# A deformable convolution with one signal for each corner of an item instead of one for each instruction

## The chip, the core and the metric

The kernel runs on one core of one Trainium2 chip. Its time is the device time of one execution in microseconds; 1330.88 us is the median of the three runs of the kernel before. The core has five engines that run their own instruction streams and tell each other of finished work by counters (semaphores): TensorE (PE, its weight loads PEld), VectorE (DVE), ScalarE (ACT), GpSimd (POOL) and SyncE (SP). An instruction can add one to a counter when it ends (here called a signal), and can wait until a counter has reached a value.

## The reference: what is computed

The input x is 4 images of 128 channels, 48 by 48, in float32. Layer 0 is a deformable 3x3 convolution behind a group normalisation, with a batch normalisation, a ReLU and a residual addition; layer 1 is a plain 3x3 convolution behind a second group normalisation, with a residual addition.

```python
x = x + _L0_conv_ref(_gn(x), ...)      # deformable convolution
x = x + _L1_conv_ref(_gn(x), ...)      # plain 3x3 convolution

# inside _L0_conv_ref, for 9 taps k and every output position
om = conv3x3(x, w_offset) + b_offset   # 27 channels: 9 dy, 9 dx, 9 masks
mask = sigmoid(om[:, 18:])
py = dy + (row + ky - 1);  px = dx + (column + kx - 1)
y0, x0 = floor(py), floor(px);  ly, lx = py - y0, px - x0
cols = corner(y0, x0, (1-ly)*(1-lx)) + corner(y0, x0+1, (1-ly)*lx) \
     + corner(y0+1, x0, ly*(1-lx))   + corner(y0+1, x0+1, ly*lx)
cols = cols * mask
out = einsum('bckhw,ock->bohw', cols, wk) + b_conv
y = relu(gamma * (out - mean) / sqrt(var + eps) + beta)   # mean, var over images and positions
```

## The kernel before, in words

The 4 x 2304 positions of layer 0 are cut into 24 **chunks** of 384 positions, each of three tiles of 128 positions (a tile's positions lie on the 128 partitions). The work of a chunk is cut into 9 **items**. In chunks 1 to 22 an item is one tap with its three tiles; in the first and the last chunk it is one tile with three taps (the last has ten). A pair of tap and tile is a **unit**, so an item has three units.

One unit passes through these steps:

- POOL gathers, by an indirect DMA (line 299), 128 rows of 4 x 128 floats from a table in DRAM: the four corners of every position, 256 KB. The row numbers come from `idx`.
- ACT multiplies the first corner by its weight into the PSUM buffer `PA` (`scale_item`, line 557, signal `scaled`).
- DVE adds the other three corners with their weights (`lerp_item`, line 770, signal `lerped`): corners 1 and 2 back into `PA`, corner 3 into `acc` in SBUF. It goes corner by corner and, in each, unit by unit, so that an item is nine instructions; each of the last six waits for the signal of the same unit's corner before.
- PE turns the 128x128 result round (`turn_item`, line 403, signal `turned`) into the PSUM buffer `TP`.
- ACT copies the three turned tiles to `cols` (`copy_cols`, line 538, signal `copied`).
- PE multiplies them with the weights of the tap into `CO` (`conv_item`, line 392, signal `conved` once an item).

The buffers `PA`, `TP` and `cols` are double, `acc` is triple. The order on each engine is fixed by the loops. ACT runs, for item k, `scale_item(k)` and then `copy_cols(k-1)`. DVE runs `lerp_item(k)`. PE runs `turn_item(k)` and then `conv_item(k-1)`. In the first three items of a chunk PE also computes, ahead of the turn, three taps of the next chunk's offset convolution (line 352, 27 channels into `OMT`).

The next chunk's row numbers come out of the present chunk's middle: after item 3 PE turns the offsets (line 361), and after `lerp_item(4)` DVE runs `indices` (lines 708 to 744), 18 small instructions that give `idx` (line 717), the corner weights `wt` and the sums `vsum`. POOL waits for `idx` before it gathers the next chunk's 27 units; each of its gathers also waits until the same place of `g` has been used (`lerped`). After item 1 ACT copies the previous chunk's output (`copy_out`, line 548), which waits for `conved`. `copy_cols` waits for `turned` of its item and for `conved` of the item two before (line 537), since it overwrites that item's half of `cols`. `copy_v` (line 530) copies a small transposed tile to `vt` after item 6 and also waits for `conved`.

After the last chunk come the batch statistics, the ReLU, the second normalisation and layer 1 (lines 477 and 860 to 871).

## Time and profile before

| what | value |
|---|---|
| median of 3 runs (lowest, highest) | 1330.88 us (1327.02, 1339.39) |
| the profiled execution's own time | 1331.31 us |
| its span | 1329.6 us |
| PE busy | 783.9 us (59%) |
| DVE busy | 687.7 us (52%) |
| POOL busy | 669.0 us (50%) |
| ACT busy | 369.8 us (28%) |
| mean granted TensorE clock | 0.721 of full speed |

No engine is busy for more than 59% of the span. Such a kernel is bound by the chain of who waits for whom, and not by the work of one engine, so the views that matter are those of the waits and of the order in time.

### The profile page before, as it was taken

Reading aid. Unit: us, or ns where it says so; the run is one execution under the profiler, and the core shown is the slowest. Engines: PE = TensorE matmul, PEld = TensorE weight load, DVE = VectorE, ACT = ScalarE, POOL = GpSimd, SP = SyncE. Lnnn points to the kernel's source line nnn. Section 1 sums busy time; section 2 is a strip of 40 time slices with the busy share of each in tenths; the row PEclk is TensorE's granted clock in tenths of the full one; section 3 lists DMA queues with packets and bytes.
Section 4 is the critical chain, followed back from the end, with each engine's and each line's share of the span. In section 5 each row is a group of like instructions: output and inputs, shape, how many; then the busy total and the mean of one; then the engine's idle time right before and its main releaser. Section 6 shows DMA issues by size and latency. Waiting matters only on the chain.

```text
span 1329.6 us, 10583 instructions
## 1 busy us (share of the span) xinstructions
PE 783.9 (59%) x2380; PEld 376.8 (28%) x2380; DVE 687.7 (52%) x2662; ACT 369.8 (28%) x1026; POOL 669.0 (50%) x731
## 2 busy tenths in 40 slices
PE   7463646655555544656555544656555556555999
PEld 4232222222122222222122122222122122135777
DVE  4337446446447446446437536536436436465664
ACT  3213224223213214313213214313213213234320
POOL 4374374373473474374464465364364364361743
PEclk8665766767766767767776767767777677666999
DMA  7364464363473374373474364374364364360011
GB/s 282 118 183 126 118 199 117 111 201 108 119 206 108 116 209 117 104 208 108 116 204 114 117 197 129 99 199 120 104 203 123 107 198 127 104 176 22 37 53 54
DMA packets 55971, 181.50 MB, mean 137 GB/s; under 512 B 10980, under 2 KB 11492, under 8 KB 55524
## 3 DMA queue, kind: packets, MB, share of 16 engines
q0 software_dynamic: 51840, 169.91, 44.4%
q1 hardware_dynamic: 3780, 10.32, 2.1%
q10 hardware_dynamic: 288, 0.59, 0.1%
q14 instruction: 43, 0.35, 0.1%
q8 instruction: 20, 0.33, 0.1%
HBM read 176.06 MB, written 4.72 MB: 136 GB/s over the span
## 4 chain that ended last, share of the span: by engine, by line
another core or an unknown queue 27%; PE 22%; issue 21%; DVE 19%; ACT 10%; DMA 1%; POOL 1%; ACTq 0%; DVEq 0%; SPq 0%
DVE PA L770 10%; ACT PA L557 8%; PE OMT L352 5%; PE CO L392 5%; DVE acc L770 5%; PE TP L403 4%; PE TP L477 2%; PE PA L477 2%; PE CO L477 2%; ACT cols L538 1%; PE OMT L477 1%; PE VU L477 1%; DMA g<-corner_table,idx 1%; DVE bst L688 1%
## 5 line engine op out<-in xcount | busy, mean ns | idle before, releaser
L299 POOL DMA_INDIRECT g<-corner_table,idx x648 | 612.7, 946 | 581.4 <-DVE idx L717 366.2
L770 DVE SCALAR_TENSOR_TENSOR PA<-g,wt,PA 128x128 f32<-128x128 f32 x1296 | 358.0, 349 | 496.4 <-ACT PA L557 300.0
L403 PE MATMUL TP<-ident,acc 128*128 128x128 f32 x648 | 157.4, 367 | 398.4 <-DVE acc L770 216.8
L392 PE MATMUL CO<-cols,wcs 128*128 128x384 f32 (+1 forms) x504 | 266.1, 637 | 130.0 <-issue 100.1
L538 ACT ACTIVATE cols<-TP 128x384 f32<-128x384 f32 (+1 forms) x217 | 104.9, 484 | 736.8 <-remote 364.3
L403 PEld LDWEIGHTS TP<-ident,acc 128*128 128x128 f32 x648 | 90.2, 178 | 533.7 <-DVE acc L770 280.7
L352 PE MATMUL OMT<-xn,woff 128*27 128x384 f32 (+2 forms) x450 | 231.0, 671 | 1.2 <-ACT mask L519 0.7
L770 DVE SCALAR_TENSOR_TENSOR acc<-g,wt,PA 128x128 f32<-128x128 f32 x648 | 191.5, 342 | 63.5 <-DVE acc L770 36.5
L557 ACT ACTIVATE PA<-g,wt 128x128 f32<-128x128 f32 x648 | 203.3, 358 | 9.8 <-DMA g<-corner_table,idx 8.9
L392 PEld LDWEIGHTS CO<-cols,wcs 128*128 128x128 f32 x504 | 109.8, 279 | 160.1 <-issue 113.6
L352 PEld LDWEIGHTS OMT<-xn,woff 128*27 128x27 f32 x450 | 55.7, 138 | 177.7 <-issue 174.9
L245 POOL TENSOR_TENSOR g<-xn 128x288 f32<-128x288 f32 (+1 forms) x60 | 41.9, 731 | 34.3 <-ACT xn L623 33.2
L378 PE MATMUL CO<-vt,ut 9*128 9x384 f32 (+1 forms) x56 | 32.2, 666 | 0.0
L237 POOL TENSOR_TENSOR x<-x,o 128x576 f32<-128x576 f32 x8 | 11.5, 1454 | 23.1 <-ACT o L617 23.0
L530 ACT ACTIVATE vt<-VU 9x384 f32<-9x384 f32 x24 | 11.5, 478 | 32.4 <-issue 15.1
L367 PE MATMUL VU<-ident,vsum 128*9 128x128 f32 x72 | 17.7, 374 | 2.6 <-issue 2.6
L523 ACT ACTIVATE std<-OMT,eps 128x1 f32<-128x1 f32 x5 | 1.3, 261 | 59.4 <-PE OMT L335 59.4
L519 ACT ACTIVATE mask<-OMT 128x27 f32<-128x27 f32 (+2 forms) x25 | 4.8, 192 | 46.0 <-DVE pos L709 43.2
L548 ACT ACTIVATE o<-CO,params 128x384 f32<-128x384 f32 x23 | 13.2, 575 | 13.2 <-remote 12.8
L477 PE MATMUL OMT<-g,w 128*128 128x288 f32 x48 | 14.6, 444 | 2.2 <-DVE g L245 2.2
L496 ACT ACTIVATE xn<-x,gshift,gscale 128x1872 f32<-128x1872 f32 (+3 forms) x9 | 10.8, 1236 | 17.8 <-DVE gshift L682 11.1
L367 PEld LDWEIGHTS VU<-ident,vsum 128*9 128x9 f32 x72 | 9.1, 128 | 20.1 <-issue 18.6
(119 smaller groups left out, 495.7 us busy)
## 6 DMA issues: line engine op xcount, KB each, us to landing
g<-corner_table,idx POOLq DMA_INDIRECT x648
out_dram<-x SPq DMA_DIRECT2D x16, 288.0 KB, 2.1
x<-x_dram SPq DMA_DIRECT2D x3, 1152.0 KB, 8.1
wconv<-wconv_dram SPq DMA_DIRECT2D x1, 576.0 KB, 5.2
w<-w_dram SPq DMA_DIRECT2D x1, 576.0 KB
x<-x_dram ACTq DMA_DIRECT2D x1, 384.0 KB, 5.0
x<-x_dram SPq DMA_DIRECT2D x1, 384.0 KB, 4.7
x<-x_dram ACTq DMA_DIRECT2D x1, 192.0 KB, 3.5
```

Of the source, the lines that this page charges most:

```text
L245: return eng.tensor_tensor(mixed[:, m, first:first + rows, :], p, q, op)
L299: pl.indirect_dma_start(out=g[:, k, t].rearrange("p q c -> p (q c)"), out_offset=None, in_=tab_d, in_offset=bass.IndirectOffsetOnAxis(ap=i ...
L352: last = nc.tensor.matmul(OM[:, first * W:(first + rows) * W], woff[:, k, :], xn[:, row + k // 3:row + k // 3 + rows, k % 3:k % 3 + W], st ...
L367: last = nc.tensor.transpose(VT[:, t * P:(t + 1) * P], vsum[:, t, :], ident[:])
L378: nc.tensor.matmul(co_bank(c, t)[:, lo:hi], ut[:, c // CHUNKS % 2, :], vt[:, lo:hi], start=True, stop=False)
L392: last = nc.tensor.matmul(co_bank(c, t)[:, t * P:t * P + size], wcs[:, c // CHUNKS % 2, k, :], cols[:, s % 2, n * P:n * P + size], start=F ...
L403: last = nc.tensor.transpose(TP[s % 2][:, n * P:(n + 1) * P], acc[:, s % 3, n, :], ident[:])
L477: last = nc.tensor.matmul(MX[h % 2][m][:, 0:HB], w, mixed[:, m, r:r + BR, :], start=(ky == 0), stop=(ky == 2))
L538: nc.scalar.activation(cols[:, s % 2, 0:size], TP[s % 2][:, 0:size], ACT.Copy).then_inc(copied, 1)
L557: nc.scalar.activation(PA[s % 2][:, n * P:(n + 1) * P], g[:, k, t, 0, :], ACT.Copy, scale=wt[:, c % 2, 0, t, k:k + 1]).then_inc(scaled, 1)
L688: nc.vector.bn_stats(bst[:, j, :], x[:, b * HW + j * CP:b * HW + (j + 1) * CP]).then_inc(stats_in, 1)
L770: nc.vector.scalar_tensor_tensor(acc[:, s % 3, n, :] if q == 3 else a, g[:, k, t, q, :], wt[:, c % 2, q, t, k:k + 1], a, ALU.mult, ALU.add ...
```

## The change

The change cuts the number of signals and of the waits that go with them. No arithmetic instruction is added or dropped.

- `lerp_item` signals once for each corner of an item (3 signals) and no longer once for each instruction (9). A corner's first instruction waits for the last instruction of the corner before. Over the kernel the `lerped` signals go from 1944 to 651.
- `scale_item` signals once an item (`scaled`, from 648 to 217).
- `conv_item` signals once a chunk, with the last tap, and once a tile in the last chunk (`conved`, from 217 to 26). `copy_cols` and `copy_v` no longer wait for `conved`: PE works in order, so the turn for which they wait implies the multiplication before it.
- `indices` signals in 6 steps where it had 15 (12 for the first part); `edge`, `inside` and `vm` are computed ahead of the weights `wt`.
- `copy_v(1)` moves from chunk 0's item 7 to chunk 1's item 0.

```diff
             def conv_item(c, i):
...
-                last.then_inc(conved, 1)
+
+                if k == TAPS - 1 and (c == ALL - 1 or t == TILES - 1 or len(runs) == 1):
+                    last.then_inc(conved, 1)
 
             def turn_item(c, i):
...
-                pe.wait_ge(lerped, units_before(c, i + 1) * LERP)
+                pe.wait_ge(lerped, (s + 1) * LERP)
...
             def copy_v(c):
                 act.wait_ge(v_turned, c + 1)
-                if c:
-
-                    act.wait_ge(conved, first_item(c - 1) + (1 if c - 1 not in BY_TILE else (TILES - 1) * len(TAP_SETS) + 1))
...
             def copy_cols(c, i):
...
+
                 act.wait_ge(turned, s + 1)
-                if s > 1:
-                    act.wait_ge(conved, s - 1)
...
             def copy_out(c):
-                act.wait_ge(conved, first_item(c + 1))
+                act.wait_ge(conved, c + 1)
...
             def scale_item(c, i):
...
-                    act.wait_ge(lerped, (units_before(c, i - 1) if i else units_before(c - 1, len(items(c - 1)) - 1)) * LERP)
+                    act.wait_ge(lerped, (s - 1) * LERP)
                 for n, (k, t) in enumerate(items(c)[i]):
-                    nc.scalar.activation(PA[s % 2][:, n * P:(n + 1) * P], g[:, k, t, 0, :], ACT.Copy,
-                                         scale=wt[:, c % 2, 0, t, k:k + 1]).then_inc(scaled, 1)
+                    last = nc.scalar.activation(PA[s % 2][:, n * P:(n + 1) * P], g[:, k, t, 0, :], ACT.Copy, scale=wt[:, c % 2, 0, t, k:k + 1])
+                last.then_inc(scaled, 1)
...
-                    if ahead and k == 7:
+                    if ahead and k == 7 and c:
                         copy_v(c + 1)
+                    if c == 1 and k == 0:
+
+                        copy_v(1)
...
             def lerp_item(c, i):
...
-                dve.wait_ge(scaled, done + len(units))
+                dve.wait_ge(scaled, s + 1)
                 for q in range(1, 4):
+                    if q > 1:
+                        dve.wait_ge(lerped, s * LERP + q - 1)
+                    if q == 3 and s > 2:
+                        dve.wait_ge(turned, s - 2)
                     for n, (k, t) in enumerate(units):
-                        if q > 1:
-                            dve.wait_ge(lerped, done * LERP + (q - 2) * len(units) + n + 1)
-                        if q == 3 and n == 0 and s > 2:
-                            dve.wait_ge(turned, s - 2)
                         a = PA[s % 2][:, n * P:(n + 1) * P]
-                        nc.vector.scalar_tensor_tensor(acc[:, s % 3, n, :] if q == 3 else a, g[:, k, t, q, :],
-                                                       wt[:, c % 2, q, t, k:k + 1], a, ALU.mult, ALU.add).then_inc(lerped, 1)
+                        last = nc.vector.scalar_tensor_tensor(acc[:, s % 3, n, :] if q == 3 else a, g[:, k, t, q, :],
+                                                              wt[:, c % 2, q, t, k:k + 1], a, ALU.mult, ALU.add)
+                    last.then_inc(lerped, 1)
```

In `indices` the instructions stay the same 18; the order on DVE in chunk 1 is shown from `rest` on, with the first rows of the item behind it. Before:

```order
L721 TENSOR_SCALAR rest<-less_frac 128x54 [waits index_step]
L723 TENSOR_TENSOR my<-mask,rest 128x27 [waits mask_ready,index_step]
L725 SCALAR_TENSOR_TENSOR my<-mask,less_frac 128x27
L730 TENSOR_TENSOR wt<-my,rest 128x27 [waits index_step]
L728 SCALAR_TENSOR_TENSOR wt<-my,less_frac 128x27
L730 TENSOR_TENSOR wt<-my,rest 128x27
L728 SCALAR_TENSOR_TENSOR wt<-my,less_frac 128x27
L739 TENSOR_SCALAR edge<-pos 128x54
L740 SCALAR_TENSOR_TENSOR inside<-pos,edge 128x54 [waits index_step]
L741 SCALAR_TENSOR_TENSOR vm<-inside,mask 128x27 [waits index_step]
L744 SCALAR_TENSOR_TENSOR vsum<-inside,vm 128x27 [waits v_turned,index_step]
L770 SCALAR_TENSOR_TENSOR PA<-g,wt,PA 128x128 [waits scaled,gathered5]
```

The same place of DVE in the changed kernel, as far as the end of the item behind the indices:

```order
L710 TENSOR_SCALAR rest<-less_frac 128x54 [waits index_step]
L713 SCALAR_TENSOR_TENSOR inside<-pos,edge 128x54
L717 TENSOR_TENSOR my<-mask,rest 128x27 [waits index_step,mask_ready]
L718 SCALAR_TENSOR_TENSOR my<-mask,less_frac 128x27
L720 SCALAR_TENSOR_TENSOR vm<-inside,mask 128x27
L727 TENSOR_TENSOR wt<-my,rest 128x27 [waits index_step]
L725 SCALAR_TENSOR_TENSOR wt<-my,less_frac 128x27
L732 SCALAR_TENSOR_TENSOR vsum<-inside,vm 128x27 [waits v_turned]
L757 SCALAR_TENSOR_TENSOR PA<-g,wt,PA 128x128 [waits scaled,gathered5]
L757 SCALAR_TENSOR_TENSOR PA<-g,wt,PA 128x128 [waits lerped]
L757 SCALAR_TENSOR_TENSOR acc<-g,wt,PA 128x128 [waits turned,lerped]
```

`inside` and `vm` have moved ahead of the weights (the second pair of `wt` rows, which repeats the first, is not shown), four waits are left in these rows where there were six, and each corner of the item has one wait.

On ACT, at the border of chunks 0 and 1 (item 7 of chunk 0 to item 1 of chunk 1), the copy of `vt` moves. Before:

```order
L538 ACTIVATE cols<-TP 128x384 [waits conved,turned]
L530 ACTIVATE vt<-VU 9x384 [waits conved,v_turned]
L557 ACTIVATE PA<-g,wt 128x128 [waits lerped,gathered8]
L557 ACTIVATE PA<-g,wt 128x128 [waits lerped,gathered0,wt_ready]
L557 ACTIVATE PA<-g,wt 128x128 [waits lerped,gathered1]
L548 ACTIVATE o<-CO,params 128x384 [waits conved]
```

The changed kernel, the same stretch of ACT:

```order
L550 ACTIVATE PA<-g,wt 128x128 [waits lerped,gathered8]
L531 ACTIVATE cols<-TP 128x384 [waits turned]
L550 ACTIVATE PA<-g,wt 128x128 [waits lerped,gathered0,wt_ready]
L524 ACTIVATE vt<-VU 9x384 [waits v_turned]
L550 ACTIVATE PA<-g,wt 128x128 [waits lerped,gathered1]
L541 ACTIVATE o<-CO,params 128x384 [waits conved]
```

The copy of `vt` now stands after chunk 1's first products, and of ACT's waits for `conved` only the one of `copy_out` is left.

## Rows read from the trace of the kernel before

**Rows 1.** The page: busy, 40 slices of POOL, and lines (count | busy us, mean ns)

```profile
PE 783.9 (59%) x2380; PEld 376.8 (28%) x2380; DVE 687.7 (52%) x2662; ACT 369.8 (28%) x1026; POOL 669.0 (50%) x731
...
POOL 4374374373473474374464465364364364361743
...
L299 POOL DMA_INDIRECT g<-corner_table,idx x648 | 612.7, 946 | 581.4 <-DVE idx L717 366.2
```

**Rows 2.** Waits of the whole span: engine, line <- releaser: total us, times, longest

```profile
POOL g L299 <- DVE idx L717: 366.2, 23, 18.1
ACT cols L538 <- remote: 364.3, 38, 17.6
```

**Rows 3.** Timeline, POOL: start, us, instruction, count, idle before

```profile
364.53 0.94 POOL L299 DMA_INDIRECT g<-corner_table,idx  x1 [15.49 <-DVE idx L717]
...
397.01 0.95 POOL L299 DMA_INDIRECT g<-corner_table,idx  x1 [0.30 <-issue]
414.60 0.94 POOL L299 DMA_INDIRECT g<-corner_table,idx  x1 [16.65 <-DVE idx L717]
```

**Rows 4.** That chunk in stretches: PE, PEld, DVE, ACT, POOL, clock, DMA share

```profile
366.00:374.00 8.00, 5.24 (x16) 3.04 (x17) 7.27 (x29) 2.11 (x7) 6.17 (x7) 0.60 0.67 200
374.00:400.00 26.00, 12.81 (x28) 4.05 (x28) 7.60 (x27) 3.78 (x12) 18.17 (x20) 0.70 0.74 211
400.00:414.00 14.00, 10.70 (x30) 3.89 (x30) 8.07 (x33) 5.36 (x17) 0.00 (x0) 0.69 0.00 1
```

**Rows 5.** Timeline, PE and ACT, early in that burst of gathers

```profile
368.62 0.90 PE L403 MATMUL TP<-ident,acc 128*128 128x128 f32 x3 [3.90 <-DVE acc L770]
...
369.56 0.49 ACT L538 ACTIVATE cols<-TP 128x384 f32<-128x384 f32 x1 [3.46 <-issue]
```

**Rows 6.** Timeline, PE, ACT and DVE, late in that burst

```profile
377.69 0.79 PE L403 MATMUL TP<-ident,acc 128*128 128x128 f32 x3 [2.56 <-DVE acc L770]
378.66 0.49 ACT L538 ACTIVATE cols<-TP 128x384 f32<-128x384 f32 x1 [3.54 <-PE TP L403]
383.58 0.35 DVE L770 SCALAR_TENSOR_TENSOR acc<-g,wt,PA 128x128 f32<-128x128 f32 x1 [1.03 <-DVE acc L770]
387.10 0.55 PE L403 MATMUL TP<-ident,acc 128*128 128x128 f32 x3 [2.28 <-remote]
391.28 0.49 ACT L538 ACTIVATE cols<-TP 128x384 f32<-128x384 f32 x1 [11.29 <-remote]
391.67 0.94 ACT L557 ACTIVATE PA<-g,wt 128x128 f32<-128x128 f32 x3
402.59 0.49 ACT L538 ACTIVATE cols<-TP 128x384 f32<-128x384 f32 x1 [9.98 <-remote]
```

**Rows 7.** The chain of waits there: start, us, what (L537 waits for conved)

```profile
382.89 0.02 ACTq L537
...
396.89 0.02 ACTq L537
```

**Rows 8.** Timeline, DVE and ACT, late in the next burst

```profile
435.06 0.35 DVE L770 SCALAR_TENSOR_TENSOR PA<-g,wt,PA 128x128 f32<-128x128 f32 x1 [3.52 <-remote]
436.46 0.35 DVE L770 SCALAR_TENSOR_TENSOR PA<-g,wt,PA 128x128 f32<-128x128 f32 x1 [1.04 <-issue]
...
446.26 0.49 ACT L538 ACTIVATE cols<-TP 128x384 f32<-128x384 f32 x1 [16.77 <-remote]
```

**Rows 9.** Timeline, DVE, after the burst of rows 3

```profile
411.13 1.65 DVE L770 SCALAR_TENSOR_TENSOR PA<-g,wt,PA 128x128 f32<-128x128 f32 x6 [1.44 <-ACT PA L557]
412.69 0.86 DVE L770 SCALAR_TENSOR_TENSOR acc<-g,wt,PA 128x128 f32<-128x128 f32 x3
...
414.15 0.19 DVE L717 SCALAR_TENSOR_TENSOR idx<-low,row 128x27 int32<-128x27 f32 x1
```

**Rows 10.** Timeline, the first burst: PE and ACT

```profile
29.87 0.90 PE L403 MATMUL TP<-ident,acc 128*128 128x128 f32 x3 [1.25 <-DVE acc L770]
...
45.74 0.49 ACT L538 ACTIVATE cols<-TP 128x384 f32<-128x384 f32 x1 [16.06 <-remote]
```

More of the change, by code:

```diff
@@ L50, in first_item @@
     return sum(len(items(i)) for i in range(c))
-def units_before(c, i):
-    return c * TAPS * TILES + sum(len(units) for units in items(c)[:i])
 def last_use(c, unit):
@@ L68, in pos_step @@
 def pos_step(part):
-    return (SHORT_STEPS + (part - 1) * STEPS if part else 0) + 2
+    return part * STEPS + 1
 def landed(c, i):
@@ L296, in _ @@
                             used = max(used, i)
-                        pl.wait_ge(lerped, units_before(c - 1, used + 1) * LERP)
+                        pl.wait_ge(lerped, (first_item(c - 1) + used + 1) * LERP)
                     for k, t in units:
@@ L502, in scale_weights @@
                 if b > 1:
-                    act.wait_ge(conved, first_item((b - 1) * CHUNKS))
+                    act.wait_ge(conved, (b - 1) * CHUNKS)
                 nc.scalar.activation(wcs[:, b % 2].rearrange("p k c -> p (k c)"), wconv[:].rearrange("p k c -> p (k c)"),
@@ L541, in copy_out_tile @@
                 lo, hi = t * P, (t + 1) * P
-                act.wait_ge(conved, first_item(ALL) if t == TILES - 1 else first_item(ALL - 1) + (t + 1) * len(TAP_SETS))
+                act.wait_ge(conved, ALL + t)
                 nc.scalar.activation(o[:, (ALL - 1) * CP + lo:(ALL - 1) * CP + hi], co_bank(ALL - 1, t)[:, lo:hi],
@@ L690, in statistics @@
                 aggregate(CHUNKS)
-            steps = [0]
             def indices(c, part, lo=0, hi=TILES):
-                def step(ins):
-                    steps[0] += 1
-                    ins.then_inc(index_step, 1)
-                    dve.wait_ge(index_step, steps[0])
-                assert steps[0] + 2 == pos_step(part)
-                s = steps[0]
+                s = part * STEPS
                 b, j = divmod(c, CHUNKS)
@@ L712, in indices @@
                 dve.wait_ge(index_step, s + 2)
-                nc.vector.tensor_scalar(pos[:, n], pos[:, n], -1.0, float(H), ALU.max, ALU.min).then_inc(index_step, 1)
+                nc.vector.tensor_scalar(row[:, n], low[:, n, 0:9], -ROUND, float(SIDE), ALU.add, ALU.mult).then_inc(index_step, 1)
+                if whole:
+                    nc.vector.tensor_scalar(edge[:], pos[:], -1.0, float(H), ALU.mult, ALU.add)
                 dve.wait_ge(index_step, s + 3)
-                nc.vector.tensor_scalar(row[:, n], low[:, n, 0:9], -ROUND, float(SIDE), ALU.add, ALU.mult).then_inc(index_step, 1)
@@ L716, in indices @@
-                dve.wait_ge(index_step, s + 5)
                 nc.vector.scalar_tensor_tensor(idx[:, c % 2, n], low[:, n, 9:18], float(b * TABLE + SIDE + 1) - ROUND, row[:, n], ALU.add, ALU.add).then_inc(idx_ready, 1)
                 nc.vector.scalar_tensor_tensor(less_frac[:, n], low[:, n], -ROUND, pos[:, n], ALU.add, ALU.subtract).then_inc(index_step, 1)
-                steps[0] = s + 6
-                dve.wait_ge(index_step, s + 6)
-                step(nc.vector.tensor_scalar(rest[:, n], less_frac[:, n], 1.0, None, ALU.add))
@@ L722, in indices @@
-                dve.wait_ge(mask_ready, part + 1)
-                nc.vector.tensor_tensor(my[:, 0, n], mask[:, n], rest[:, n, 0:9], ALU.mult).then_inc(index_step, 1)
-                steps[0] += 1
-                step(nc.vector.scalar_tensor_tensor(my[:, 1, n], mask[:, n], -1.0, mv_y, ALU.mult, ALU.mult))
+                dve.wait_ge(index_step, s + 4)
+                last = nc.vector.tensor_scalar(rest[:, n], less_frac[:, n], 1.0, None, ALU.add)
+                if whole:
+                    last = nc.vector.scalar_tensor_tensor(inside[:], pos[:], 1.0, edge[:], ALU.add, ALU.min)
@@ new lines, in indices @@
+                last.then_inc(index_step, 1)
+                dve.wait_ge(mask_ready, part + 1)
+                dve.wait_ge(index_step, s + 5)
+                nc.vector.tensor_tensor(my[:, 0, n], mask[:, n], rest[:, n, 0:9], ALU.mult)
+                last = nc.vector.scalar_tensor_tensor(my[:, 1, n], mask[:, n], -1.0, my_y, ALU.mult, ALU.mult)
+                if whole:
+                    last = nc.vector.scalar_tensor_tensor(vm[:], inside[:, :, 0:9], 1.0, mask[:], ALU.min, ALU.mult)
+                last.then_inc(index_step, 1)
@@ L734, in indices @@
                 last.then_inc(wt_ready, 1)
-                if hi < TILES:
-                    return
-                step(nc.vector.tensor_scalar(edge[:], pos[:], -1.0, float(H), ALU.mult, ALU.add))
-                step(nc.vector.scalar_tensor_tensor(inside[:], pos[:], 1.0, edge[:], ALU.add, ALU.min))
-                step(nc.vector.scalar_tensor_tensor(vm[:], inside[:, :, 0:9], 1.0, mask[:], ALU.min, ALU.mult))
-                if c:
-                    dve.wait_ge(v_turned, c)
-                nc.vector.scalar_tensor_tensor(vsum[:], inside[:, :, 9:18], 1.0, vm[:], ALU.min, ALU.mult).then_inc(v_ready, 1)
+                if whole:
+                    if c:
+                        dve.wait_ge(v_turned, c)
+                    nc.vector.scalar_tensor_tensor(vsum[:], inside[:, :, 9:18], 1.0, vm[:], ALU.min, ALU.mult).then_inc(v_ready, 1)
```

17 lines of the change are left out of this document (7 added, 10 removed).

## Prediction

> **What bounds the kernel now.** The page comes first [rows 1]: no engine is busy for more than 59%, and POOL's slices swing between 3 and 7 tenths with a period of two to three slices, so POOL works in bursts. The waits say what stands between them [rows 2]: POOL waits 366.2 us, 23 times, for `idx` of the next chunk, 15.9 us each. This is the largest wait that stands in a loop: the row numbers are due after item 4, item 4 needs its gathers, and the gathers need the row numbers.
>
> The timeline of one chunk gives the loop's parts [rows 3]. 27 gathers (648 in 24 chunks [rows 1]) are issued from 364.53 to 397.96, 33.4 us or 1.25 us each, and the next burst begins at 414.60. A turn of the loop is 50.1 us here and 49.3 on average: (33.4 + 0.3) of issuing + 15.9 of waiting, less rounding. 24 such turns are 1183 us of the 1330.
>
> Why is item 4 late? Not from work. The three stretches of the chunk [rows 4] show VectorE busy for 7.27 of the first 8 us, for 7.60 of the next 26, and for 8.07 of the last 14, when the DMA is idle. In the middle stretch, in which the gathers land, all engines but POOL do next to nothing.
>
> What they wait for is a message that has been sent already. Early in the burst, PE's turn ends at 369.52 and ACT's copy starts at 369.56 [rows 5]. Late in the burst the same pair comes apart [rows 6]. The turn of item 8 ends at 378.48 and its copy starts at 391.28, 12.8 us later; the turn of item 0 ends at 387.65 and its copy starts at 402.59, 14.9 us later. ACT had nothing else to run, and the profile calls the releaser "remote" since it finds none near. PE's other message, `conved`, stands between them: the chain shows ACT's waits for it ending at 382.89 and 396.89 [rows 7]. So, as I read it, PE's messages reach ACT one by one, in the order sent: `turned` 378.66, `conved` 382.89, `turned` 391.28, `conved` 396.89, `turned` 402.59. The gaps are 4.2, 8.4, 5.6 and 5.7 us. VectorE's own messages come late too, at another rate: in the next burst its instructions start 1.40 us apart, of which 0.35 is work [rows 8]. Also PE's turn at 387.10 starts 3.2 us after the last sum has ended at 383.93 [rows 6]. Copies on "remote" waits sum to 364.3 us over the span [rows 2]. This late phase begins some 10 us after the burst's start (turn 7's copy, 378.66, is the first late one) and ends with its last gathers. Items 2, 3 and 4 are then done in the 14 us behind it.
>
> The Trainium skill, "TensorE: Matmul & The Clock Gate", section "The cost: per-tile semaphore tail", says that increments of TensorE go one after another, at 26.3 ns each. By it the 191 `conved` signals dropped would be worth 5 us in all; the rows show the same order, one after another, but gaps of microseconds.
>
> **The change part by part.** The sums are made against the profiled execution, 1331.3 us; the median of the runs is 1330.9, so no correction is due.
>
> *conved, once a chunk.* In a late phase the messages of PE to ACT are halved: of the five above two are `conved`. One is left, behind the turn of item 0, for `copy_out`. I lay out the same burst with the same openings (378.66, 382.89, 391.28, 396.89, 402.59), now taken by turned 7, turned 8, turned 0, the one `conved`, turned 1. The copy of item 0 runs at 391.3 and not at 402.6. `copy_out` and item 2's products then go at 396.9 to 398.4 (0.94 the products [rows 6]) and its sums to 401.0 (2.5 us an item [rows 9]). Item 3 starts behind the opening at 402.6: copy and products to 403.9, sums to 406.5. Item 4's sums follow to 409.0, and `idx`, 0.6 us behind them as now (413.55 to 414.15 [rows 9]), comes at 409.6 and not at 414.15: 4.5 us a turn, 23 turns, **104 us**. If PE's messages pass at the shortest gap seen, 4.2 us, the same layout gives turned 0 at 387.1, `conved` at 391.3, turned 1 at 395.5 and turned 2 at 399.7, so item 4's products to 401.0, its sums to 403.6 and `idx` at 404.2: 9.9 us a turn, **228 us**.
>
> *lerped, three an item.* VectorE sends 3 messages where it sent 9, and has two waits on itself where it had six. Where its messages come 1.4 us apart, nine of them need 12.6 us and three need 4.2. Whether its crowd is also what holds PE's messages up can't be read from one kernel. For it: in the next burst, where VectorE's instructions stand 1.40 us apart, ACT's copy waits 16.8 us [rows 8], against 11.3 and 10.0 in rows 6. Against it: in the first burst the turn of item 0 ends at 30.77 and its copy starts at 45.74 [rows 10], though VectorE had only the 18 messages of items 0 and 1 to send by then. So the price is placed between the two layouts, at their mean: **7 us a turn**.
>
> *The coarser wait.* In an item's sums six instructions take 1.65 us, so they start 0.26 apart and last 0.35 [rows 9]. Now the first of a corner waits for the end of the last: 0.35 - 0.26 = 0.09 more twice an item, plus the message's way, for which I take 0.03 (369.52 to 369.56 in rows 5 is 0.04). Items 2 to 4 behind the burst pay it on the path: 3 x 2 x 0.12 = 0.7 us a turn, 17 us in all. The 7 us are meant with it. Its upper bound is the idle 1.04 us of rows 8, which holds only in the late phase and has there six places now and two afterwards.
>
> *scaled, once an item.* VectorE waited for an item's last product before, and does so now: nothing. *Indices in 6 steps.* On the way to `idx` stand one wait less and one instruction more (`edge`), each under 0.19 us [rows 9]: +-4 us over 23 turns, taken as nothing. The weights come behind `edge`, `inside` and `vm`, at most 0.6 us later; ACT needs them for the next chunk's item 0, four items on: nothing, while those four items' work covers it. *copy_v(1)* runs behind chunk 1's item 0 products; PE needs `vt` an item later: nothing.
>
> *The sum.* 23 x 7 = 161 us, so 1331 - 161 = **1170 us**. The stages after the last chunk, some 115 us, don't change.
>
> **The rivals.**
>
> *A. The late phase goes altogether* (its cause is the crowd of messages, and two thirds of VectorE's and nearly half of PE's are gone). Then `idx` is ready before POOL has finished a burst, and the turn is POOL's 33.7 us: 366 us less [rows 2], 965. The next bound is close: PE is busy for 28.8 us in the 48 us of rows 4, VectorE for 22.9. With some waits left, 965 to 1055, taken as 1010. For it: early in the burst, with VectorE busy for 7.27 of 8 us [rows 4] and signalling each instruction, nothing is late, so the path itself can carry the traffic. Against it: rows 10.
>
> *B. Nothing moves.* The lateness belongs to the DMA's traffic, and ends with it whatever is sent: in the first burst PE's messages pass at 45.7 and then after the end. Items 2 to 4 still run behind the burst, 1331, or a few us less. A rule of signals that cost nothing gives the same time: if the wait of 12.8 us in rows 6 were something other than a late message, dropping messages would free nothing. The Trainium skill, "VectorE: DVE Perf Modes", section "The DRAIN you can't avoid", measured eight copies with a semaphore after each and with one after the last and found no difference; early in the burst this trace agrees (0.26 us a start, each with a signal), late in it the trace does not (1.40 us).
>
> *C. Slower.* As B, and the coarser wait is bare. Before, corner 2 of a unit waited for a message sent two instructions earlier; now it waits for one sent just now. Behind the burst this is the 0.7 us a turn, 17 us: 1348. If in the late phase each of the two waits shows 1.4 us and VectorE is on the path there, two items add 5.6 us less the 1.4 that they lose now [rows 6], so up to 4 us a turn and 1420. It decides if PE's openings come no earlier than now, for then nothing pays for it. I take 1350.
>
> *D. A small gain*: the openings are as now in half the bursts and never better: 1.5 to 3 us a turn, 1260 to 1300.
>
> **How the numbers follow.** The forecast, partial relief with 1100 to 1255 as its own range, has 0.42. A has 0.23, D 0.12, B 0.12, C 0.11. The likeliest case gives the time, 1170. For 8 in 10 the range takes in all of the forecast and D, most of A and B: 990 to 1338; left out are the fastest third of A, a little of B and most of C, 0.2 together. This kernel's runs lie within 1% of each other, so 1% is what can be told from no change. Faster by over 1% (under 1318): 0.42 + 0.23 + 0.12 = 0.77. Within 1%: 0.13. Slower: 0.10.
>
> **What would show it.** In the profile after, POOL's 23 waits for `idx` should be 9 us each and not 15.9, their sum some 205; under A below 40, under B 366. ACT's copies on "remote" should fall from 364 to under 200. PE's turn and ACT's copy late in a burst should be 4 to 6 us apart, under B still 12 to 15. VectorE's sums of an item should take 2.7 us where nothing is late, against 2.4 now; if they take more than 3.5 late in the bursts and POOL's waits are not shorter, it is C. The forecast is wrong if openings turn out to be set by the transfers alone, or if they vanish once VectorE is quiet.

## The result, and the profile after

The changed kernel takes **1343.9 us** (median of 10 runs, 1340.4 to 1345.3) against 1331.4 for the kernel before (10 runs): ratio **1.0085**, interval 1.0069 to 1.0102. It is slower by a little under one per cent. The forecast was 1170 us, and its range ended at 1338. The profiled execution took 1340.4 us, with a span of 1338.5; before it was 1329.6.

The page of the kernel after, in the lines that answer to [rows 1]: busy time, POOL's slices, the line of the gathers.

```profile
PE 781.8 (58%) x2380; PEld 374.6 (28%) x2380; DVE 713.1 (53%) x2662; ACT 369.8 (28%) x1026; POOL 669.5 (50%) x731
POOL 4364374464374364364364365364364364361743
L294 POOL DMA_INDIRECT g<-corner_table,idx x648 | 613.1, 946 | 589.1 <-DVE idx L707 372.5
```

The waits after, as in [rows 2] (total us, times, longest).

```profile
ACT cols L531 <- remote: 418.8, 42, 15.2
POOL g L294 <- DVE idx L707: 372.5, 23, 17.4
```

POOL still waits 16 us, 23 times, for the next chunk's row numbers (372.5 us, 366.2 before), and ACT's copies wait longer for messages that the profile finds no near sender for (418.8 us, 364.3 before). VectorE's busy time rose by 25.4 us. The prediction had named 205 us and under 200 us for these two waits. The timeline of POOL over one turn of the loop, after, answers to [rows 3].

```profile
365.63 0.94 POOL L294 DMA_INDIRECT g<-corner_table,idx  x1 [17.34 <-DVE idx L707]
...
398.12 0.95 POOL L294 DMA_INDIRECT g<-corner_table,idx  x1 [0.31 <-issue]
415.10 0.94 POOL L294 DMA_INDIRECT g<-corner_table,idx  x1 [16.03 <-DVE idx L707]
```

The same burst, 27 gathers 1.25 us apart, and the same pause behind it. The stretches of that chunk after (columns as in [rows 4]):

```profile
367.00:375.00 8.00, 4.98 (x14) 2.71 (x15) 7.53 (x27) 1.82 (x5) 6.17 (x7) 0.50 0.69 197
375.00:401.00 26.00, 14.43 (x33) 4.44 (x31) 7.74 (x27) 3.98 (x12) 18.28 (x20) 0.70 0.72 211
401.00:415.00 14.00, 8.10 (x25) 3.65 (x26) 9.18 (x37) 6.16 (x19) 0.00 (x0) 0.74 0.01 2
```

In the 26 us of the middle VectorE again does 27 instructions, 7.74 us of work (7.60 before). The late phase is still there. PE's turns and ACT's copies in it, after, as in [rows 6], two views of one stretch:

```profile
379.22 0.55 PE L400 MATMUL TP<-ident,acc 128*128 128x128 f32 x3 [2.47 <-issue]
384.66 0.55 PE L400 MATMUL TP<-ident,acc 128*128 128x128 f32 x3 [0.55 <-remote]
```

```profile
376.90 0.49 ACT L531 ACTIVATE cols<-TP 128x384 f32<-128x384 f32 x1 [0.52 <-issue]
387.45 0.49 ACT L531 ACTIVATE cols<-TP 128x384 f32<-128x384 f32 x1 [9.22 <-issue]
403.60 0.49 ACT L531 ACTIVATE cols<-TP 128x384 f32<-128x384 f32 x1 [14.82 <-remote]
```

The turn of item 8 ends at 379.77 and is copied at 387.45, 7.7 us later. The turn of item 0 ends at 385.21 and is copied at 403.60, 18.4 us later. Before, the two were 12.8 and 14.9 us [rows 6]. Between these two turns PE now sends no `conved`; the only one left, for `copy_out`, comes behind the turn of item 0. So item 8's message did pass 5.1 us sooner after its turn, but item 0's passed no sooner. Its copy starts 4.5 us behind the end of the burst's last gather (403.60 against 399.07), where it was 4.6 us [rows 3, rows 6]. In 20 of the 21 turns of chunks 1 to 21 it is 4.5 to 4.7 us, in both kernels.

**One thing is needed to read the experiments.** The runs come in series, each on one chip (the expectations say "call"). In some series the kernel before took 1331 to 1345 us, in others 950 to 951 us: same program, same data. Where it took 951 us the late phase was missing. One chip showed 951 us in one series and 1331 us in a later one. So each experiment is compared only with the runs of the kernel before in its own series, and I name the series "with late messages" and "without".

### The profile page after: what moved, and what is told of

It reads as the page before. It is cut to its first block, busy times and chain, and to the rows that moved or that the text cites. A ratio compares the mean times of both kernels' runs of the same rounds, so it can differ in the third digit from the quotient of the medians.

```text
span 1338.5 us, 10322 instructions
## 1 busy us (share of the span) xinstructions
PE 781.8 (58%) x2380; PEld 374.6 (28%) x2380; DVE 713.1 (53%) x2662; ACT 369.8 (28%) x1026; POOL 669.5 (50%) x731
## 4 chain that ended last, share of the span: by engine, by line
another core or an unknown queue 30%; PE 22%; DVE 19%; issue 19%; ACT 9%; POOL 1%; DMA 1%; DVEq 0%; ACTq 0%; POOLq 0%
DVE PA L757 9%; ACT PA L550 6%; PE OMT L347 6%; DVE acc L757 4%; PE CO L387 4%; PE TP L400 3%; PE TP L474 2%; PE PA L474 2%; PE CO L474 2%; ACT cols L531 1%; PE OMT L474 1%; PE VU L474 1%; POOL g L294 1%; DVE bst L684 1%
## 5 line engine op out<-in xcount | busy, mean ns | idle before, releaser
L294 POOL DMA_INDIRECT g<-corner_table,idx x648 | 613.1, 946 | 589.1 <-DVE idx L707 372.5
L757 DVE SCALAR_TENSOR_TENSOR PA<-g,wt,PA 128x128 f32<-128x128 f32 x1296 | 376.0, 351 | 487.9 <-ACT PA L550 236.5
L531 ACT ACTIVATE cols<-TP 128x384 f32<-128x384 f32 (+1 forms) x217 | 105.2, 485 | 746.8 <-remote 418.8
L757 DVE SCALAR_TENSOR_TENSOR acc<-g,wt,PA 128x128 f32<-128x128 f32 x648 | 186.9, 344 | 56.8 <-remote 30.2
L342 PE MATMUL PA<-gavg 128*128 128x128 f32 x90 | 13.8, 318 | 2.8 <-POOL gavg L275 2.6
```

Source lines behind the costliest of these rows:

```text
L294: pl.indirect_dma_start(out=g[:, k, t].rearrange("p q c -> p (q c)"), out_offset=None, in_=tab_d, in_offset=bass.IndirectOffsetOnAxis(ap=i ...
L342: nc.tensor.matmul(PA[0][:, 0:P], gavg[:], gavg[:], start=True, stop=True)
L531: nc.scalar.activation(cols[:, s % 2, 0:size], TP[s % 2][:, 0:size], ACT.Copy).then_inc(copied, 1)
L757: last = nc.vector.scalar_tensor_tensor(acc[:, s % 3, n, :] if q == 3 else a, g[:, k, t, q, :], wt[:, c % 2, q, t, k:k + 1], a, ALU.mult, ...
```

## The experiments

### One part of the change at a time

Theories: (T1) the forecast, PE's messages pass one by one at openings, and fewer of them pass earlier; (T2) lateness is unmoved and the coarser wait costs what rival C said. Three kernels in a series with late messages, kernel before 1345.3 us. (The expectations number their theories each in its own way.)

**lerp_only**: the kernel before, with one signal for each corner of an item.

```diff
+                    if q > 1:
+                        dve.wait_ge(lerped, s * LERP + q - 1)
+                    if q == 3 and s > 2:
+                        dve.wait_ge(turned, s - 2)
                     for n, (k, t) in enumerate(units):
-                        if q > 1:
-                            dve.wait_ge(lerped, done * LERP + (q - 2) * len(units) + n + 1)
-                        if q == 3 and n == 0 and s > 2:
-                            dve.wait_ge(turned, s - 2)
...
+                        last = nc.vector.scalar_tensor_tensor(...)
+                    last.then_inc(lerped, 1)
```

> The kernel before, with one part of the change alone: the sums of an item signal once for each corner (651 signals, not 1944), and each corner's first instruction waits for the last of the corner before. Theory 1 (the coarser wait is the whole loss, and it is paid behind each burst): an item's sums take 2.66 us where nothing is late, not 2.43; items 2 to 4 pay it, 0.7 us a turn, so 1331 + 12 to 17 = 1343 to 1348, ratio 1.009 to 1.013, as the whole change or a little worse. Theory 2 (the loss comes from somewhere else, PE's signals or the indices): within 0.3% of before. Rival, my forecast's idea that VectorE's crowd of signals holds PE's up: 20 us or more faster.

Measured: 1361.3 us, ratio 1.012 (1.010 to 1.014), 16 us slower. Its waits:

```profile
ACT cols L538 <- remote: 409.8, 45, 17.6
POOL g L299 <- DVE idx L717: 386.0, 23, 19.1
```

Two thirds of VectorE's signals of the sums are gone, and POOL waits longer than in conv_only below (370.8 us), whose time is that of the kernel before. So the number of these signals is not what holds PE's messages up.

**conv_only**: the kernel before, with `conved` once a chunk, ACT's waits on it dropped, and `copy_v(1)` moved.

```diff
-                last.then_inc(conved, 1)
+                if k == TAPS - 1 and (c == ALL - 1 or t == TILES - 1 or len(runs) == 1):
+                    last.then_inc(conved, 1)
...
-                if s > 1:
-                    act.wait_ge(conved, s - 1)
```

> The kernel before, with PE's part of the change alone: the multiplications of a chunk signal once, the copies on ACT no longer wait for them, and the copy of vt for chunk 1 moves. The forecast's layout (PE's messages pass at fixed openings, one each, so that a conved less lets a turned through earlier) expects 104 us less, about 1227. Theory 1 (an item's turned message passes when the transfers allow it, whatever else PE has sent) expects 0 to 5 us less, ratio 0.996 to 1.000.

Measured: 1344.3 us, ratio 0.9992 (0.9974 to 1.0009). The 104 us of the fixed openings do not come. Its waits:

```profile
POOL g L299 <- DVE idx L715: 370.8, 23, 18.8
ACT cols L534 <- remote: 370.7, 42, 19.7
```

**nine_sums**: the changed kernel, with nine signals an item and the wait of each instruction back.

```diff
+                        if q > 1:
+                            dve.wait_ge(lerped, done * LERP + (q - 2) * len(units) + n + 1)
...
-                    last.then_inc(lerped, 1)
+                        nc.vector.scalar_tensor_tensor(acc[:, s % 3, n, :] if q == 3 else a, g[:, k, t, q, :],
+                                                       wt[:, c % 2, q, t, k:k + 1], a, ALU.mult, ALU.add).then_inc(lerped, 1)
```

> The changed kernel with the sums' nine signals and per-instruction waits put back; the rest of the change stays. Theory 1 (coarser wait is the loss): back to 1326 to 1332, ratio 0.996 to 1.001. Theory 2 (the loss lies in the indices, the single scaled signal or PE's part): stays near 1343, ratio 1.009.

Measured: 1351.0 us, ratio 1.0035 (1.0023 to 1.0048) against the kernel before, between the two expected values. So something other than the sums costs some 5 us too, and `conved` is not it.

**indices_only** (a later series with late messages, kernel before 1343.5): the kernel before with the change's indices.

```diff
-                nc.vector.scalar_tensor_tensor(low[:, n], ot[:, n, 0:18], -0.5, grid[:, j, n], ALU.add, ALU.add).then_inc(index_step, 1)
+                nc.vector.scalar_tensor_tensor(low[:, n], ot[:, n, 0:18], -0.5, grid[:, j, n], ALU.add, ALU.add)
...
+                if whole:
+                    nc.vector.tensor_scalar(edge[:], pos[:], -1.0, float(H), ALU.mult, ALU.add)
```

> The kernel before with the indices of the change alone (6 steps, edge, inside and vm ahead of the weights). In the traces so far idx starts 0.82 us behind item 4's last sum in the changed kernel and 0.61 us in the kernel before. On a chip with late messages this stands on the path of 23 turns: 23 x 0.21 = 4.8 us, ratio 1.003 to 1.004; rival: the indices cost nothing and the 0.35% of the kernel with nine sums lie in the single scaled signal, ratio 0.999 to 1.001. On a chip without late messages: idx is ready before POOL wants it, ratio 1.000.

Measured: 1350.3 us, ratio 1.0048 (1.0032 to 1.0064): 6.4 us by the ratio. The timelines tell where. VectorE, the kernel before, the steps ahead of the `idx` of [rows 9]:

```profile
413.46 0.21 DVE L708 SCALAR_TENSOR_TENSOR low<-OMT,grid 128x54 f32<-128x54 f32 x1
413.70 0.19 DVE L711 TENSOR_SCALAR low<-low 128x54 f32<-128x54 f32 x1
413.93 0.18 DVE L715 TENSOR_SCALAR row<-low 128x27 f32<-128x27 f32 x1
```

And VectorE in the changed kernel:

```profile
413.74 0.21 DVE L697 SCALAR_TENSOR_TENSOR low<-OMT,grid 128x54 f32<-128x54 f32 x1
413.87 0.20 DVE L698 SCALAR_TENSOR_TENSOR pos<-grid,OMT 128x54 f32<-128x54 f32 x1
414.10 0.19 DVE L700 TENSOR_SCALAR low<-low 128x54 f32<-128x54 f32 x1
...
414.42 0.18 DVE L703 TENSOR_SCALAR row<-low 128x27 f32<-128x27 f32 x1
...
414.64 0.19 DVE L707 SCALAR_TENSOR_TENSOR idx<-low,row 128x27 int32<-128x27 f32 x1
```

Before, `idx` starts 0.69 us after `low` (413.46 to 414.15), after it 0.90 us. Before, each step waited for an instruction one further back; with one signal for two instructions it waits for the one just issued: `low` to its clip is 0.24 us before and 0.36 after, the clip to `row` 0.23 and 0.32. 23 x 0.21 = 4.8 us, all on the path: POOL's burst starts when `idx` is there.

### What the lateness depends on

Theories: the bytes of the gathers; the number of PE's messages; the rate at which POOL issues gathers. Four kernels, each the kernel before with one edit.

```diff
# bytes_quarter: gather 512 B a row and not 2 KB (bytes_half: 0:2 and c=2 * P, 1 KB)
-    out=g[:, k, t].rearrange("p q c -> p (q c)"), out_offset=None, in_=tab_d,
+    out=g[:, k, t, 0:1].rearrange("p q c -> p (q c)"), out_offset=None, in_=tab_d.rearrange("r (h c) -> (r h) c", c=1 * P),
...
# more_signals: two more signals of PE an item, on a counter nobody reads
+    if n < len(units) - 1:
+        last.then_inc(spare, 1)
# paced2: two small memsets on POOL behind each gather
+    pl.memset(pad[:, 0:70], 0.0).then_inc(paced, 1)
...
+    pl.memset(pad[:, 70:140], 0.0).then_inc(paced, 1)
```

The kernels with fewer bytes gather one or two corners and sum them again in the place of the others, so their result is another. The first series came **without** late messages (kernel before 951.0 us), so it tells what these edits cost where nothing is late.

> The kernel before with gathers of half the bytes: 1 KB a row and not 2 KB, from rows of a half as long; the sums read corners 0 and 1 twice, so the result is another. POOL issues as many gathers at the same pace, with as many rows and completions. Theory 1 (late messages come from the bytes that the gathers move: the DMA engines are at 0.72 in a burst): the DMA share in a burst falls to about 0.4, the copies late in a burst start at once, POOL's wait for idx falls from 15.9 us a turn to under 3, and the time from 1331 to 960 to 1050. Theory 2 (they come from POOL's issuing or from the number of descriptors and completions): the late phase stays and the time is within 3% of before.

Measured 950.6, ratio 0.9993 (0.9982 to 1.0003).

> As the kernel with half the bytes, with a quarter: 512 bytes a row, and the sums read corner 0 three times more; the result is another. Theory 1 (bytes): late messages gone, time as with half the bytes or a little less, POOL's 33.7 us a turn being the bound, 960 to 1000. Theory 2 (issuing or descriptors): within 3% of before. If half the bytes help in part and a quarter more, the lateness grows with the load and has no edge.

Measured 949.3, ratio 0.9982 (0.9967 to 0.9996).

> The kernel before with two more signals an item from PE: the first and second turn of an item add to a counter for which nobody waits, so PE sends four messages an item and not two. The forecast's layout (messages pass one by one at fixed openings) expects the copies late in a burst to come later still, items 0 and 1 to fall behind the burst: 5 to 10 us a turn, 1450 to 1560. If the number doesn't matter, as the kernel with PE's part of the change alone suggests: within 0.5% of before.

Measured 952.3, ratio 1.0004 (0.9994 to 1.0013).

> The kernel before with two small memsets on POOL behind each gather, so that gathers follow each other every 1.6 to 1.9 us and not every 1.25: a burst takes 43 to 51 us and the DMA share in it falls from 0.72 to 0.48 to 0.57. If late messages come from the DMA's load and vanish under it, a turn becomes POOL's own 43 to 51 us with idx always ready: between 160 us faster and 30 us slower, and POOL's waits for idx fall under 3 us each. If they come from the burst being there at all (whatever its rate), items 2 to 4 still wait for the burst's end, and a turn is 43 to 51 + 16 us: 1550 to 1750.

Measured 1030.3, ratio 1.0828 (1.081 to 1.0846). All four expectations were built on a kernel of 1331 us, and they are void as tests of the lateness. What they show is the other limit: without it the loop is POOL's issuing, and pacing only costs. For half the bytes there is no run with late messages; the other three edits have one.

A second series, again without late messages (kernel before 950.4), had the changed kernel in it:

> The changed kernel once more, beside the kernel before on the chip of this call. The last call's chip ran the kernel before in 951 us, with none of the late messages; the call before had one that takes 1345. On a chip with late messages: ratio 1.007 to 1.011 as the first time. On one without: a turn is POOL's 33.8 us, the coarser wait and the longer indices hide behind POOL but for the first and last chunk and the start, so 0 to 3 us slower on 951, ratio 1.000 to 1.003.

Measured 952.0, ratio 1.0007 (0.9994 to 1.0019). The same series repeated three of the edits.

> The kernel before with a quarter of the gathered bytes (512 bytes a row, the sums read corner 0 three times more; the result is another), again, for a chip with late messages. Theory 1 (the bytes of a burst make messages late): 945 to 1000 us where the kernel before takes 1330 to 1345. Theory 2 (POOL's issuing, or the number of rows and completions): within 3% of before. On a chip without late messages: as before, 0.998, as the last time.

> The kernel before with two more signals an item from PE for which nobody waits, again, for a chip with late messages. The forecast's fixed openings, one message each: 5 to 10 us a turn more, 1450 to 1560. If the number of PE's messages doesn't matter: within 0.5% of before. On a chip without late messages: 1.000, as the last time.

> The kernel before with two small memsets on POOL behind each gather, again, for a chip with late messages (without them it took 1030 us against 951). If lateness comes from load and goes when the gathers are a tenth to a third further apart: 1030 to 1060 us against 1330 to 1345. If it comes from a burst being there at any rate: 1400 to 1450, since a turn is then 37 + 13 to 16 us.

They gave 0.9957 (0.9944 to 0.9971), 1.0002 (0.9992 to 1.0012) and 1.0803 (1.0779 to 1.0827). The changed kernel without late messages, POOL's timeline at the seam of two bursts:

```profile
255.15 0.95 POOL L294 DMA_INDIRECT g<-corner_table,idx  x1 [0.30 <-issue]
256.40 0.95 POOL L294 DMA_INDIRECT g<-corner_table,idx  x1 [0.30 <-issue]
```

256.40 is already the next chunk's first gather: there is no pause. Stretches of that burst (columns as in [rows 4]):

```profile
222.00:232.00 10.00, 5.70 (x17) 3.33 (x18) 8.67 (x36) 3.44 (x11) 7.55 (x9) 0.52 0.72 211
232.00:256.00 24.00, 17.29 (x55) 6.72 (x53) 18.99 (x76) 10.95 (x34) 18.21 (x20) 0.85 0.73 211
```

The transfers are as dense as in the late runs (share 0.73, 211 GB/s; 0.74 and 211 in [rows 4]), but VectorE does 76 instructions in 24 us and not 27 in 26. Its PE and ACT there:

```profile
240.06 0.55 PE L400 MATMUL TP<-ident,acc 128*128 128x128 f32 x3
```

```profile
240.65 0.49 ACT L531 ACTIVATE cols<-TP 128x384 f32<-128x384 f32 x1 [2.89 <-PE TP L400]
```

The turn ends at 240.61 and the copy starts 0.04 us later, late in a burst.

The third series had late messages (kernel before 1343.5).

> The kernel before with a quarter of the gathered bytes (the sums read corner 0 three times more; the result is another), for a chip with late messages. Bytes are the cause: 945 to 1000 us against 1330 to 1345. POOL's issuing, or the number of rows and completions: within 3% of before. On a chip without late messages: 0.996 to 0.998, as twice before.

Measured 1343.0, ratio 0.9987 (0.9974 to 1.0). A stretch late in its burst, and a turn and its copy in the same one:

```profile
382.00:406.00 24.00, 13.42 (x31) 4.41 (x29) 7.42 (x27) 3.62 (x12) 18.01 (x20) 0.78 0.18 52
```

```profile
391.55 0.55 PE L403 MATMUL TP<-ident,acc 128*128 128x128 f32 x3 [1.14 <-remote]
...
410.56 0.49 ACT L538 ACTIVATE cols<-TP 128x384 f32<-128x384 f32 x1 [14.20 <-remote]
```

The DMA share fell from 0.74 to 0.18, and the turn that ended at 392.10 is still copied only at 410.56, 18.5 us later. **Bytes are not the cause.**

> The kernel before with two more signals an item from PE for which nobody waits, for a chip with late messages. Fixed openings, one message each: 1450 to 1560. If the number of PE's messages doesn't matter, as PE's part of the change alone says (0.9992): within 0.5% of before. On a chip without late messages: 1.000, as twice before.

Measured 1344.5, ratio 1.0006 (0.9995 to 1.0017). With conv_only this closes the question of the number of PE's messages: 191 fewer, or two more an item, and no change.

> The kernel before with two small memsets on POOL behind each gather, for a chip with late messages. On the two chips without them a burst took 37 us and the kernel 1028 to 1030 us against 951. If lateness goes with a lower load: 1030 to 1060 us against 1330 to 1345, so that it beats both kernels there. If any burst makes it: 1400 to 1450.

Measured 1255.2, ratio **0.9341** (0.9325 to 0.9357). POOL's timeline and the waits of that kernel:

```profile
299.07 0.95 POOL L302 DMA_INDIRECT g<-corner_table,idx  x1 [0.15 <-issue]
300.03 0.17 POOL L308 MEMSET pad<- 128x70 f32 x1
300.12 0.17 POOL L312 MEMSET pad<- 128x70 f32 x1
300.44 0.95 POOL L302 DMA_INDIRECT g<-corner_table,idx  x1 [0.15 <-issue]
```

```profile
ACT cols L549 <- remote: 406.1, 52, 14.4
POOL g L302 <- DVE idx L728: 209.8, 23, 12.6
```

A gather each 1.37 us and not 1.25 makes POOL slower and the kernel faster: POOL's wait for `idx` is 210 us, against 376 us in more_signals_3 of the same series. Of the three causes tried, the rate of the gathers is the one that moves the lateness. It doesn't make single messages less late, it makes the late phase begin later. In the mean, item 8 is copied 1.3 us behind its turn (11.6 in the kernel before), item 0 8.4 us (11.8) and item 1 15.3 us (3.8). So one more item gets through during the burst.

### The rate, further

**paced4** and **paced4_change** have four memsets behind each gather, on the kernel before and on the changed one; the series had late messages, kernel before 1330.8 us.

> The kernel before with four memsets behind each gather: one gather every 1.57 us, a burst of 42.5 us. If the lateness falls with the rate and is gone here, a turn is POOL's 42.7 us and the time 1150 to 1165, on a chip with late messages and on one without. If it stays as with two memsets: a turn is 42.5 + 9.3, 1380.

Measured 1178.1, ratio **0.8852** (0.882 to 0.8884). POOL's timeline and the largest wait of ACT:

```profile
299.94 0.95 POOL L302 DMA_INDIRECT g<-corner_table,idx  x1
...
301.51 0.95 POOL L302 DMA_INDIRECT g<-corner_table,idx  x1
```

```profile
ACT PA L576 <- DMA g<-corner_table,idx: 506.6, 183, 4.7
```

At 1.57 us a gather the late copies are gone: ACT now waits for gathers, 2.8 us each, and in the mean turn `idx` is ready 13 us before POOL asks for it. The loop is POOL's issuing again, 43.4 us a turn.

> The changed kernel with the same four memsets behind each gather. Where late messages are gone, the fewer signals and the coarser waits both hide behind POOL: within 0.3% of the paced kernel without the change. If some lateness is left, the coarser waits and the later idx cost 0.5 us a turn as they do unpaced: 0.5 to 1% slower than it. Rival: with a lower rate the number of VectorE's messages begins to matter, and the changed kernel is more than 1% faster than it.

Measured 1179.6, ratio 0.8863 (0.8831 to 0.8895). The change is worth nothing here too, as without late messages.

**paced3_2**: three memsets. Its series came without late messages (kernel before 950.1).

> The kernel before with three small memsets on POOL behind each gather, between two (a gather every 1.37 us: 1255 us, POOL's wait for idx 9.3 us a turn) and four (1.57 us: 1178 us, the wait under 1 us). A gather every 1.47 us, a burst of 39.8 us. If the lateness has an edge between 1.37 and 1.47 us: a turn of 40.1 us, 1331 - 23 x 9.3 = 1110 to 1125, the fastest kernel on such a chip. If it falls evenly with the rate: a wait of 4 to 5 us, a turn of 44.5, 1205 to 1220, slower than with four. On a chip without late messages: 1090.

Measured 1118.2, ratio 1.1768 (1.1749 to 1.1788), so it can't tell whether the lateness ends at once between 1.37 and 1.57 us or evenly. It took more than was expected for this case (1090): a turn is 40.9 us, the burst 39.95 of it.

### The mean turn

Worked out from the timelines of each profiled execution, means over the bursts of chunks 1 to 21, in us. A turn of the loop is a burst (first gather to the end of the last) and the pause behind it; "at" counts from the first gather.

| kernel | turn | burst | pause | item 0 copied at | item 2's sums at | items 2 to 4 | sums of an item | last sum to `idx` |
|---|---|---|---|---|---|---|---|---|
| before | 49.50 | 33.44 | 16.06 | 37.33 | 39.88 | 8.55 | 2.41 | 0.61 |
| after | 49.85 | 33.46 | 16.38 | 36.76 | 39.26 | 9.30 | 2.68 | 0.82 |
| lerp_only | 50.49 | 33.52 | 16.97 | 37.84 | 40.26 | 9.16 | 2.68 | 0.61 |
| conv_only | 49.80 | 33.53 | 16.27 | 37.74 | 40.21 | 8.50 | 2.41 | 0.64 |
| nine_sums | 50.36 | 33.52 | 16.84 | 37.44 | 40.07 | 9.00 | 2.41 | 0.83 |
| indices_only | 50.34 | 33.48 | 16.85 | 37.64 | 40.11 | 8.94 | 2.41 | 0.83 |
| more_signals_3 | 50.02 | 33.45 | 16.57 | 37.70 | 40.19 | 8.77 | 2.41 | 0.61 |
| paced2_3 | 46.26 | 36.91 | 9.34 | 27.52 | 31.07 | 13.73 | 2.41 | 0.99 |
| paced4 | 43.42 | 42.37 | 1.05 | 12.26 | 17.15 | 11.98 | 2.41 | 0.74 |

The rows come from four series, in which the kernel before took 1331.4 us (before, after), 1345.3 (lerp_only, conv_only, nine_sums), 1343.5 (indices_only, more_signals_3, paced2_3) and 1330.8 (paced4). The turns of one execution scatter by about 1 us, so within a series lerp_only is best read against conv_only, and indices_only against more_signals_3, whose times are those of the kernel before. A copy's lateness, from the end of PE's turn to ACT's copy, is in the mean, before: 11.8 (item 0), 11.6 (item 8), 3.8 (item 1), 3.2 (item 7); after: 14.3, 9.3, 6.7, 1.6; the changed kernel without late messages: 0.05 for item 0.

## Why the prediction was wrong

**What bounds the kernel: right.** The loop of POOL's burst and the pause behind it, with items 2 to 4 done in the pause, is what both kernels show, and paced2_3 shows that a shorter pause shortens the kernel, though its burst is 3.5 us longer. The profile of before also had the right cause of the pause, PE's message of item 0, long sent.

***conved*, once a chunk: the step that failed.** It laid the same five openings under fewer messages and took 4.5 us a turn, 104 us, from that. The opening times were fitted to five events of one burst and taken for a property of the path, which a message fewer would use better. conv_only measured 0.9992 (-1 us) and more_signals_3 1.0006. The layout had item 0's copy at 391.3, within the burst. In the changed kernel it is 4.5 to 4.7 us behind the burst's last gather in 20 of 21 turns, as before, whatever was sent ahead of it. The copies of items 7 and 8 did come sooner (1.6 and 9.3 us behind their turns, 3.2 and 11.6 before), and that gained nothing, since item 2 waits for item 0's copy. That the openings might be "set by the transfers alone" stood among the ways to be wrong; rival B had it, at 0.12. B's own reason, the DMA's traffic, is right only as far as the gathers' rate goes: their bytes don't matter (0.9987 at a quarter).

The Trainium skill, "TensorE: Matmul & The Clock Gate", section "The cost: per-tile semaphore tail", gives, as an estimate from its 26.3 ns an increment, 5 us for the 191 signals. The interval of conv_only, worked against 1345.3 us, is -3.5 to +1.2 us, so here less than that is on the path.

***lerped*, three an item: nothing gained.** It was priced between two layouts of the openings, 7 us a turn, 161 us with the step above. Alone, with its coarser wait, it costs 16 us (lerp_only), no more than the wait by itself explains. No kernel here has the fewer signals without the coarser wait, so a gain of a few us under its cost is not excluded. VectorE's own waits in the late phase did shrink in number, but what they save is not on the path: item 2 waits for item 0's copy, and the copy for the burst's end.

**The coarser wait: right in size, and on the path in part.** It was put at 2.7 us an item against 2.4; the mean of the sums is 2.68 against 2.41, 0.27 us more. VectorE behind the burst in the changed kernel:

```profile
411.15 1.77 DVE L757 SCALAR_TENSOR_TENSOR PA<-g,wt,PA 128x128 f32<-128x128 f32 x6
412.96 0.86 DVE L757 SCALAR_TENSOR_TENSOR acc<-g,wt,PA 128x128 f32<-128x128 f32 x3
```

Six instructions in 1.77 us where [rows 9] has 1.65, and the next three begin 1.81 us after the first where it was 1.56. Three items behind the burst make 3 x 0.27 x 23 = 18.6 us; predicted were 17, and lerp_only measured 16. Against conv_only its items 2 to 4 take 0.66 us more a turn, of 0.81.

**Indices in six steps: taken as nothing, is 5 to 6 us.** The count of waits and instructions was right. What it left out is how far behind its instruction each wait stands, the very thing the prediction had priced for the sums.

***scaled*, `copy_v(1)`: nothing,** as far as conv_only (which has the copy) and nine_sums (1.0035, within the interval of indices_only alone) can tell.

**The sum that stands.** The means over 21 turns mislead for the changed kernel: in the first of them (chunk 1) it starts item 2 at 26.5 us, still in the burst, and needs 18.2 us for items 2 to 4. Over the other 20 turns item 2 starts at 39.90 and not 39.97; items 2 to 4 take 8.86 us and not 8.59, +0.27; `idx` comes 0.21 later; together +0.41 a turn, 20 turns 8.2 us, against 8.9 of span. So of the 0.81 us by which the sums of three items are longer, only 0.27 is on the path: the idle time of VectorE between these sums fell from 1.37 to 0.84 us. The parts measured alone give 16 + 6.4 - 1 = 21 us, the whole 12.5. The difference lies in this idle time, as far as two profiled executions can tell, and no run here shows why it shrinks with the whole change and hardly with lerp_only (1.31 us in conv_only, 1.17 in lerp_only).

**The rivals.** C came true in its direction and, in part, in its mechanism, at 1344 where it was taken at 1350; the indices, which it took as nothing, are some 5 of the 12.5 us. A's time (965) is what the kernel takes where nothing is late: 951 and 952 for the two kernels. It was tied to the wrong cause, the crowd of messages.

## What to carry to other kernels

A wait is cheapest when it stands a few instructions behind what it waits for: joining three signals into one moved each wait right behind its instruction, and made an item's sums 0.27 us longer, while the signals dropped had cost nothing that could be measured. When a wait ends long after its sender has ended, times read from one burst tell when it ended, not by what rule; test the rule (here with more signals and with a quarter of the bytes) before a gain is built on it. A kernel whose time changes by 40% between series with no edit has a condition around it, and a cure for that condition is a loss where it is absent. Pacing the gathers gave 0.934 (two memsets) and 0.885 (four) with late messages, and 1.08 (two) and 1.18 (three) without. And look at single turns before a mean is explained: one turn of 21 made a gain that the other 20 don't have.

## What the runs showed of the hardware that was not expected

- PE's messages to ACT come up to 19 us late (in the turn of chunk 1 up to 24; VectorE's to itself about 1 us, [rows 8]) during a burst of POOL's indirect DMAs each 1.25 us. The late phase begins some 10 us into the burst, and in all but the turn of chunk 1 item 0's copy stands 4.5 to 4.7 us behind its last gather. It does not go with the bytes (time ratio 0.9987 at a quarter) nor with the number of PE's messages (0.9992 with fewer, 1.0006 with more). It goes with the rate of the gathers: 1.37 us apart 0.9341, 1.57 us apart 0.8852.
- It is absent in some series, in which the same kernel takes 951 us. One chip showed both. What sets it is open.
- Whether the lateness ends at an edge between 1.37 and 1.57 us, or evenly, is open: the kernel for it met a series without late messages.
- That it is POOL's issuing, and not the memsets themselves, that frees the messages was not separated: no kernel here paces without them. Nor was the rate of issuing separated from the number of rows: every gather here has 128 rows, so pacing spreads both.
